# Mirrored angles in the first stage of a one-core vision-transformer tower, and the maximum over the raw output matrix moved to the end of that stage

## The reference, cut to what matters

```python
# stage 1: an S4D kernel for 64 inputs c, 128 channels h, 64 modes n, 1024 steps l
dt = exp(log_dt); A = -exp(inv_A_real) + 1j * A_imag; dtA = A * dt[:, None]
Cc = B * C * (exp(dtA) - 1) / A
K  = 2 * einsum('chn,hnl->chl', Cc, exp(dtA[:, :, None] * arange(1024))).real
h  = K                                             # (64, 128, 1024)
# stage 3, for each of the 64 inputs
h = h + attention(layernorm(h), wq, wk, wv, wo)
h = h + ffn(layernorm(h), W_base, b_base, lora_A, lora_B, router, prior, active)
```

## Time and profile before

| | us |
|---|---|
| median of 3 runs (lowest, highest) | 3096.68 (3093.18, 3097.64) |
| the profiled execution: its time | 3095.41 |
| its span, first to last instruction | 3093.6 |
| stage 1: start to the barrier | 0 to 268.8 |
| stage 2 | 268.8 to 345.9 |
| stage 3 | 345.9 to 3093.6 |

### The profile page before, as it was taken

How to read it: one execution, slowest core, us unless ns; L and a number is a source line. 1 busy time by engine, 2 the same in 40 slices (tenths; PEclk the granted TensorE clock), 3 DMA queues, 4 the chain that set the end, 5 groups by cost and what they waited for, 6 DMA issues and landing times.

```text
span 3093.6 us, 62128 instructions
## 1 busy us (share of the span) xinstructions
PE 2852.0 (92%) x16986; PEld 1418.5 (46%) x16986; DVE 2500.3 (81%) x8865; ACT 1913.8 (62%) x5932; POOL 1966.9 (64%) x1722
## 2 busy tenths in 40 slices
PE   3767469999999999999999999999999999999986
PEld 2556234444444444444444444444444444444442
DVE  8996568888888888888888888888888888888872
ACT  5775356666666666666666666666666666666651
POOL 2441157667777767676777676777776776777762
PEclk9887789999999999999999999999999999999998
DMA  5887166676666666766666666666666666666751
GB/s 160 190 182 176 33 125 142 141 150 148 148 143 146 147 148 141 152 147 147 144 146 148 148 141 152 148 148 143 146 145 147 143 150 146 150 142 149 140 125 52
DMA packets 1269008, 442.53 MB, mean 143 GB/s; under 512 B 1200048, under 2 KB 1241264, under 8 KB 1268800
## 3 DMA queue, kind: packets, MB, share of 16 engines
q1 hardware_dynamic: 1268800, 440.62, 65.2%
HBM read 88.15 MB, written 67.11 MB: 50 GB/s over the span
## 4 chain that ended last, share of the span: by engine, by line
PE 38%; DVE 19%; issue 13%; POOL 10%; ACT 7%; DMA 1%; DVEq 0%; ACTq 0%; POOLq 0%; SPq 0%
PE bank_b L1437 18%; PE bank_a L1437 13%; DVE heads L1258 6%; DVE probs L1204 5%; ACT probs L1079 5%; POOL p_hl L1004 4%; POOL probs L1000 3%; PE bank_c L1437 3%; PE score L1408 2%; POOL rope_a L1010 2%; DVE share L1213 2%; POOL xy_hl L1019 1%; PE pv L1426 1%; DVE r L1286 1%; DVE zs L1366 1%
## 5 line engine op out<-in xcount | busy, mean ns | idle before, releaser
L1079 ACT ACTIVATE probs<-probs,negmax 128x128 f32<-128x128 f32 x2048 | 789.7, 387 | 268.9 <-DVE negmax L1204 268.9
L1004 POOL TENSOR_TENSOR p_hl<-probs,p_hl 128x512 f16<-128x512 f32 x512 | 614.9, 1201 | 354.6 <-ACT p_hl L1088 352.3
L1000 POOL TENSOR_TENSOR probs<-probs,rsum 128x512 f32<-128x512 f32 x512 | 556.7, 1087 | 221.7 <-DVE rsum L1215 220.1
L1437 PE MATMUL bank_a<-qkv_hi,xt 128*128 128x512 f16 x2048 | 655.7, 382 | 28.9 <-DMA xt<-xy_hl 28.9
L1204 DVE CUSTOM_DVE_ANT_0 probs<-score,table,scal 128x128 f32<-128x128 f32 x2048 | 596.5, 347 | 58.2 <-issue 56.9
L1437 PE MATMUL bank_b<-b_hi,yt 128*128 128x512 f16 x2048 | 643.1, 381 | 0.0
L1088 ACT ACTIVATE p_hl<-probs 128x512 f16<-128x512 f32 x512 | 319.8, 625 | 424.7 <-POOL probs L1000 417.2
L1258 DVE TENSOR_TENSOR heads<-rope_a,heads 128x512 f16<-128x512 f32 x320 | 402.4, 1273 | 36.5 <-ACT heads L1109 36.5
L1437 PE MATMUL bank_a<-qkv_lo,xt 128*128 128x512 f16 x1024 | 390.7, 381 | 0.0
L1437 PE MATMUL bank_b<-b_lo,yt 128*128 128x512 f16 x1024 | 390.0, 381 | 0.0
L1437 PE MATMUL bank_b<-o_lo,at_hi 128*128 128x512 f16 x1024 | 388.9, 380 | 0.0
(11 more groups left out here) (199 smaller groups left out, 4525.2 us busy)
## 6 DMA issues: line engine op xcount, KB each, us to landing
tok_h<-kout SPq DMA_DIRECT2D x64, 512.0 KB, 5.9
hin<-tok_h SPq DMA_DIRECT2D x64, 512.0 KB, 3.3
r<-tok_h SPq DMA_DIRECT2D x64, 512.0 KB, 3.5
out_dram<-r SPq DMA_DIRECT2D x64, 512.0 KB, 2.9
probs_t<-p_hl SPq DMA_TRANSPOSE x512, 2.8
xc<-in_x_dram SPq DMA_DIRECT2D x32, 128.0 KB, 4.7
raw_a<-in_L_attn_wq_dram SPq DMA_DIRECT2D x1, 4096.0 KB, 14.4
raw_b<-in_L_attn_wo_dram SPq DMA_DIRECT2D x32, 128.0 KB, 3.8
```

The lines of the kernel that those rows point to most:

```text
L1000: TT(x, x, rsum[:, u % 4].unsqueeze(2).to_broadcast([P, GR, T]), ALU.mult).then_inc(s_norm, 1)
L1004: TT(p_hl[:, u % 2, 1], probs[:, u % 4], p_hl[:, u % 2, 0], ALU.subtract).then_inc(s_plo, 1)
L1079: ins = A(probs[:, u % 4, g], probs[:, u % 4, g], ACT.Exp, bias=negmax[:, u % 4, g:g + 1], scale=-1.0, accum_out=sums[:, u % 4, g:g + 1])
L1437: ins = MM(bank, x(c), w[:, c, cols], start=(c == 0 and i == 0), stop=(c == KC - 1 and i == 2))
```

## The change

Four things change together.

1. **Mirrored angles.** The angle of a step is now taken from the middle of its part. Steps 127.5 + x and 127.5 - x have the same cosine and opposite sines, so `k` and `u` and the sine cover only the 128 upper steps (x = 0.5 to 127.5), and `v` is multiplied in two instructions: the upper half by `u`, the lower half by `u` read backwards and by a sign per partition. The table of parts is turned to the middles, for which all four parts now need a factor (before, part 0 had none), so the first tables have 10 rows of turns in place of 8 and factors 256 wide in place of 192.
2. **Order of the parts.** The parts are kept as 0, 2, 1, 3, so that partition half `e` of the products holds parts 2e and 2e+1, which lie side by side in `tok_h`: a store writes runs of 512 numbers (2 KB) where it wrote runs of 256 (1 KB). The bytes are the same.
3. **Loads of `wo`.** Four a chunk in chunks 0 to 7, none in chunks 8 to 15.
4. **Maximum over `raw_b`.** DVE takes it after its last chunk of stage 1 and POOL reduces it there; stage 2 no longer does.

```diff
+PART = (0, 2, 1, 3)
+LH = L0 // 2
+    c[0::2, C_SIGN] = 1
+    c[1::2, C_SIGN] = -1
+    c[:, C_HALF:C_HALF + L0 // 2] = np.arange(L0 // 2)[None, :] + 0.5
...
-        out_v = tok_h.rearrange("c h (q e l) -> e c h q l", e=2, l=L0)
+        out_v = tok_h.rearrange("c h (e q l) -> e c h q l", e=2, l=L0)
...
-                if exists(ch):
-                    load_wo(2 * ch)
-                    load_wo(2 * ch + 1)
+                if exists(ch) and ch < HQ // 4:
+                    for h in range(4 * ch, 4 * ch + 4):
+                        load_wo(h)
...
-            for m in range(1, L1):
-                step(TS(turns[:, 2 * m], turns[:, 0], float(m * L0), None, ALU.mult))
-                step(TS(turns[:, 2 * m + 1], turns[:, 0], float(m * L0), 0.25, ALU.mult, ALU.add))
+            for i in range(L1):
+                middle = PART[i] * L0 + LH - 0.5
+                step(TS(turns[:, 2 * i + 2], turns[:, 0], middle, None, ALU.mult))
+                step(TS(turns[:, 2 * i + 3], turns[:, 0], middle, 0.25, ALU.mult, ALU.add))
...
-                        ins = TS(k[:, h], const[:, C_L0:C_L0 + L0], tabc[:, nxt, NT - 1, h:h + 1],
+                        ins = TS(k[:, h], const[:, C_HALF:C_HALF + LH], tabc[:, nxt, NT - 1, h:h + 1],
                                  const[:, C_Q:C_Q + 1], ALU.mult, ALU.add)
...
-                        ins = STT(u[:, nxt, h], const[:, C_L0:C_L0 + L0], tabc[:, nxt, NT - 1, h:h + 1], k[:, h],
+                        ins = STT(u[:, nxt, h], const[:, C_HALF:C_HALF + LH], tabc[:, nxt, NT - 1, h:h + 1], k[:, h],
                                   ALU.mult, ALU.subtract)
...
-                    TT(v[:, r], v[:, r], u[:, r], ALU.mult).then_inc(s_v, 1)
+                    upper, lower = v[:, r, :, LH:L0], v[:, r, :, 0:LH]
+                    TT(upper, upper, u[:, r], ALU.mult)
+                    STT(lower, u[:, r, :, ::-1], const[:, C_SIGN:C_SIGN + 1], lower, ALU.mult, ALU.mult).then_inc(s_v, 1)
...
             V.tensor_reduce(w["mx"][:, 0:1], part_max[:, :], AX_X, ALU.max).then_inc(w["s_mx"], 1)
+            dve.wait_ge(w["wo_in"], 16 * HQ)
+            V.tensor_reduce(w["mx"][:, 1:2], w["raw_b"][:, :, :], mybir.AxisListType.XY, ALU.max,
+                            apply_absolute_value=True).then_inc(w["s_mx"], 1)
...
-            dve.wait_ge(s_in[1], 16 * HQ)
-            absmax(1, raw_b[:, :, :])
```

More of the change, by code:

```diff
@@ L43 @@
 C_ONE = C_OWN + 1
-C_ALL = C_ONE + 1
+C_SIGN = C_ONE + 1
+C_HALF = C_SIGN + 1
+C_ALL = C_HALF + L0 // 2
 def constants():
@@ L83, in token_kernel @@
         re = sb("re", [P, NS])
-        turns = sb("turns", [P, 8, NS])
-        whole = sb("whole", [P, 8, NS])
+        turns = sb("turns", [P, 2 + 2 * L1, NS])
+        whole = sb("whole", [P, 2 + 2 * L1, NS])
         sines = whole
@@ L88, in token_kernel @@
         th = sb("th", [P, NS])
-        wmag = sb("wmag", [P, L1 - 1, NS])
-        wre = sb("wre", [P, L1 - 1, NS])
-        wim = sb("wim", [P, L1 - 1, NS])
+        wmag = sb("wmag", [P, L1, NS])
+        wre = sb("wre", [P, L1, NS])
+        wim = sb("wim", [P, L1, NS])
+        g0 = sb("g0", [P, 2, NS])
         gre = sb("gre", [P, L1, NS])
@@ L102, in token_kernel @@
         xs = sb("xs", [P, 2, CH // 2, NS, 2])
-        u = sb("u", [P, 2, CH, L0])
-        k = sb("k", [P, CH, L0], I32)
+        u = sb("u", [P, 2, CH, LH])
+        k = sb("k", [P, CH, LH], I32)
         qb = sb("qb", [P, 1])
@@ L110, in token_kernel @@
         tmp = spare[:, 0, 0:18 * NS].rearrange("p (i n) -> p i n", n=NS)
-        mix = spare[:, 1, 0:18 * NS].rearrange("p (i m n) -> p i m n", i=6, n=NS)
+        mix = spare[:, 1, 0:6 * L1 * NS].rearrange("p (i m n) -> p i m n", i=6, n=NS)
         part_max = sb("part_max", [P, NCH])
@@ L248, in _ @@
             chunks(pool, body)
-            pool.wait_ge(w["s_mx"], 1)
-            nc.gpsimd.partition_all_reduce(w["mxa"][:, 0:1], w["mx"][:, 0:1], P,
-                                           bass.bass_isa.ReduceOp.max).then_inc(w["s_all"], 1)
+            for i in range(2):
+                pool.wait_ge(w["s_mx"], i + 1)
+                nc.gpsimd.partition_all_reduce(w["mxa"][:, i:i + 1], w["mx"][:, i:i + 1], P,
+                                               bass.bass_isa.ReduceOp.max).then_inc(w["s_all"], 1)
         @block.scalar
@@ L264, in _ @@
             step(nc.scalar.activation(th[:, :], re[:, :], ACT.Tanh, scale=0.5))
-            for m in range(1, L1):
-                step(nc.scalar.activation(wmag[:, m - 1], re[:, :], ACT.Exp, scale=float(m * L0)))
-            act.wait_ge(s_dt, 12)
+            for i in range(L1):
+                step(nc.scalar.activation(wmag[:, i], re[:, :], ACT.Exp, scale=float(PART[i] * L0)))
+            act.wait_ge(s_dt, 14)
             step(nc.scalar.activation(sines[:, :, :], turns[:, :, :], ACT.Sin, scale=TURN))
@@ L336, in _ @@
             step(TT(turns[:, :, :], turns[:, :, :], whole[:, :, :], ALU.subtract))
-            dve.wait_ge(s_at, 8)
+            dve.wait_ge(s_at, 9)
             t = [tmp[:, i] for i in range(18)]
@@ L362, in _ @@
             step(STT(t[1], t[16], 2.0, bi, ALU.mult, ALU.mult))
-            step(TT(gre[:, 0], t[0], t[1], ALU.add))
+            step(TT(g0[:, 0], t[0], t[1], ALU.add))
             step(STT(t[2], t[15], 2.0, bi, ALU.mult, ALU.mult))
             step(STT(t[3], t[16], 2.0, br, ALU.mult, ALU.mult))
-            step(TT(gim[:, 0], t[2], t[3], ALU.subtract))
-            sc = sines[:, 2:2 * L1].rearrange("p (m a) n -> p a m n", a=2)
+            step(TT(g0[:, 1], t[2], t[3], ALU.subtract))
+            sc = sines[:, 2:2 * L1 + 2].rearrange("p (m a) n -> p a m n", a=2)
             step(TT(wim[:, :], wmag[:, :], sc[:, 0], ALU.mult))
             step(TT(wre[:, :], wmag[:, :], sc[:, 1], ALU.mult))
-            g0r = gre[:, 0:1].to_broadcast([P, L1 - 1, NS])
-            g0i = gim[:, 0:1].to_broadcast([P, L1 - 1, NS])
+            g0r = g0[:, 0:1].to_broadcast([P, L1, NS])
+            g0i = g0[:, 1:2].to_broadcast([P, L1, NS])
             step(TT(mix[:, 0], g0r, wre[:, :], ALU.mult))
             step(TT(mix[:, 1], g0i, wim[:, :], ALU.mult))
-            step(TT(gre[:, 1:L1], mix[:, 0], mix[:, 1], ALU.subtract))
+            step(TT(gre[:, :], mix[:, 0], mix[:, 1], ALU.subtract))
             step(TT(mix[:, 2], g0r, wim[:, :], ALU.mult))
             step(TT(mix[:, 3], g0i, wre[:, :], ALU.mult))
-            step(TT(gim[:, 1:L1], mix[:, 2], mix[:, 3], ALU.add))
+            step(TT(gim[:, :], mix[:, 2], mix[:, 3], ALU.add))
             step(V.tensor_copy(tab_c[:, 0, 0:L1], gre[:, :]))
@@ L572, in _ @@
             nc.gpsimd.memset(keep["shift"][:, :], LSHIFT).then_inc(s_cst, 1)
[L574 to L578, removed]
+            pool.wait_ge(s_lmx, 1)
+            nc.gpsimd.partition_all_reduce(mxa[:, 2:3], mx[:, 2:3], P, bass.bass_isa.ReduceOp.max).then_inc(s_all, 1)
+            pool.wait_ge(s_lmx, 3)
             nc.gpsimd.partition_all_reduce(mxa[:, 3:5], mx[:, 3:5], P, bass.bass_isa.ReduceOp.max).then_inc(s_all, 1)
```

## The result

The changed kernel takes 3110.59 us (median of 5 runs, 3110.21 to 3114.82), the kernel before 3096.68: ratio 1.0051, interval 1.0036 to 1.0066. It is 14 us slower, where 23 us less were forecast.

| | stage 1 | stage 2 | stage 3 | two inputs in stage 3's loop | span |
|---|---|---|---|---|---|
| before | 268.8 | 77.1 | 2747.7 | 82.58 | 3093.6 |
| changed | 260.0 | 71.4 | 2777.4 | 83.60 | 3108.8 |
| difference | -8.8 | -5.7 | +29.7 | +1.02 | +15.2 |

A forecast was written before the change was run, and what follows sets the result against it. DVE was taken to bound stage 1, with a two-chunk loop through PE next. Stage 1's 18.4 us and stage 2's 4.8 off 3095.4 gave 3072.2, as a median 3073.5; range 3064 to 3082.

The forecast's parts named there:

- 89% of the span is the third, which the change leaves alone: Stage 3: taken as untouched by the change, so no time gained or lost there.
- The chance of 0.95 for faster: Whole kernel: faster than before 0.95, same 0.02, slower 0.03.
- Stage 1: 8.8 us in place of 18.4: Stage 1 as a whole: forecast 18.4 us shorter, ending at 247.9.
- the loop over two chunks closes at kps: Stage 1: DVE's `z` waits for PE's products in every second chunk, 2 to 3 us each.
- the tail: End of stage 1, from v(14) to the end of ACT's copies: 23.0 us, bounds 22.0 and 24.4.
- The pair: Stage 1, two chunks of the loop: 14.27 + 11.75 = 26.0 us, seven such pairs up to v(14).
- The products: Stage 1, PE's kps that close the loop: the slow kind at 1.2 GHz, 9.3 us.
- DVE's own part: Stage 1, DVE's work from the start of one `z` to the end of the next `v`: from 13.66 to 11.75 us.
- Both rivals on it: Stage 1, `u` read backwards: half rate, +7.6 us, 3081, chance 0.10; far more, slower than before, chance 0.04.
- Stage 2: 5.7 us in place of 4.8: Stage 2 without the maximum over `raw_b`: 4.8 us gained, limited by the load of `W_base`; bounds 4.8 and 5.86.
- The transfers: Stage 1, first half: longer runs make stores cheaper, near 6.3 us; sum 11.4 us a chunk, nothing waits, cost 0.
- the rival: Stage 1, transfers bound the first half: 13.2 us a chunk against 13.0, +2 to +5 us, 3076 to 3078, chance 0.14.

The follow-up runs named there:

- a_pad4: The changed kernel with four one-column memsets added on DVE at the end of stage 1: 3058.32 us, ratio 0.9878 to the kernel before.
- b_max: The kernel before with only the moved maximum over `raw_b` and its loads, four a chunk in the first half; angles unchanged: 3091.95 us, ratio 0.9982.

## Why the prediction was wrong

**The step that failed** is in the first paragraph: "89% of the span is the third, which the change leaves alone". The change left its lines alone, not its place in DVE's instruction stream: ten instructions more ahead of it brought the stall of each pass from 0.54 to 1.63 us (28 and 27 times) and stage 3 29.7 us, more than the whole gain. The signs were there to read: an "issue" wait of DVE once a pass ahead of `share`, 15.2 us in 28 times, tied to no engine. No rival had it. The chance of 0.95 for faster stood on causes that all lie in stages 1 and 2. Without that loss the time would have been 3096.7 - 14.5 = 3082 us, at the far end of the range even so, since stage 1 gave 9.6 us less than forecast (below).

That the stall is DVE's wait for instructions rests on four findings: it depends on the count of DVE instructions alone; the old time is back 128 instructions further on; it stands at one place of the program; and in all passes but the odd one it ends 1.7 to 2.1 us after a transfer of instructions has started. Ten instructions more between the loop's head and the boundary hide about 1 us of that.

The Trainium skill ("Runtime: NRT & Kernel Launch", Instruction fetch mechanics) says that a taken branch to a page that is no longer held forces a fetch before execution can go on. The runs agree in kind, with a stall of up to 2.1 us behind the back branch. The same section of the Trainium skill gives a block of 256 instructions in 16 KB; here 128 more instructions give back the old time, and the transfers have half that size. At 12 instructions between head and boundary the price over 968 was 0.84 us a pass, at 2 it was 1.9. Why it vanishes at 968 is worked out from the counts: the loop then ends at 968 + 379 = 1347, ahead of the boundary at 966 + 3 x 128 = 1350, so it lies in three blocks of 128, and at every other count tried in four. That it needs no transfers there is seen; what DVE holds of its program is not.

**Stage 1: 8.8 us in place of 18.4.** The mechanism was right (the loop over two chunks closes at kps, `z` waits 2.8 us in every second chunk, predicted "2 to 3"; PE stood idle 5.7 us ahead of these products, predicted 5.9), and so was the tail (v(14) ends at 234.35, ACT's last copy at 257.41: 23.06, predicted 23.0). The pair was sized too small, 27.3 for 26.0, in two terms:
- The products: 10.19 us against 9.3. I took kps(2) alone; in the same trace kps(8) took 10.20 after 4.48 of idle. The length of the wait alone does not say how long a burst takes: in a_pad4 the products took 8.86 us after 2.59 of idle and 7.17 after 2.88. What else sets it, no run here shows. Its first pair, closed by products of 8.86, took the 26.0 us forecast (57.54 to 83.53 on DVE), the next, closed by 10.14, took 27.3, and so did all behind it. So 26.0 could be had, for one pair; that the loop would settle on the slow kind was not in the forecast.
- DVE's own part: 12.19 against 11.75. `k` took 2.14 to 2.31, not 1.77: for 1024 columns less it lost 0.54 us, half of what the reduction's price per column gives. `u` was right at 2.19.

7 x 1.3 = 9.1, and v(0) ended at 43.28, not 42.9: together the 9.5 us by which v(14) is late.

**Reading backwards** cost at most 0.06 us: 1.28 us for `v`'s lower half, with one operand more, against 1.22. Both rivals on it fall.

**Stage 2: 5.7 us in place of 4.8**, within the bounds given (4.8 and 5.86), for the reason given: the next wait is that for `W_base`.

**The transfers** were hidden as forecast, for the wrong reason. I had halved the price of a store for its longer runs. Two pairs of late chunks, with the same `xc` loads and no `wo` loads: first b_max (1 KB runs), then the changed kernel (2 KB runs), DMA share and GB/s last:

```profile
184.40:212.00 27.60, 18.92 (x82) 15.94 (x81) 27.46 (x43) 22.28 (x37) 11.39 (x6) 0.88 0.71 172
```

```profile
194.88:222.15 27.27, 19.41 (x82) 15.95 (x81) 24.32 (x44) 20.03 (x37) 11.33 (x7) 0.87 0.67 165
```

27.6 x 0.71 = 19.6 against 27.27 x 0.67 = 18.3: hardly less: with the 2.1 us of the `xc` loads taken off, 16.2 for the stores of a pair against 17.5, not half. The rule of the Trainium skill ("DMA: Bandwidth & Descriptors", Specifications) that runs of 512 B and more go at line rate agrees with this better than my estimate did. The first half then needs what the rival said:

```profile
58.34:85.66 27.32, 19.38 (x82) 15.93 (x81) 24.32 (x45) 20.02 (x37) 11.45 (x7) 0.88 0.99 212
```

27.3 x 0.99 / 2 = 13.5 us a chunk, of 13.65, and still ACT waited for no store there: the angles with two loads a chunk had no shorter stage 1 (258.8 against 257.8). A share of 0.99 of the DMA engines is full, but not late.

## What to carry to other kernels

A long loop on an engine can stall for its own instructions behind the back branch; an edit anywhere ahead of it, in code that runs once, moves that stall. Count the engine's instructions ahead of the loop before and after an edit, look for "issue" waits that come once a pass, and compare two versions of a kernel at the same count modulo 128, else, as here, 50 us of chance lie over 15 of effect. The number of instruction transfers in the profile tells the good place from the others: 48 against 183. Here four memsets make the changed kernel 1.2% faster than before (3058.32, 0.9878), and 14 of them make the old one 0.8% faster with no other edit.

Where a loop of waits closes over an engine whose clock falls and rises, take its time from all its occurrences in the trace, and carry the slowest: the new loop settled on the slowest kind.

## What the runs showed of the hardware

- Stage 3 took 2778, 2727 and 2747 us with 964, 968 and 954 DVE instructions ahead of it, and 2747 with 1082.
- Its loop of 379 DVE instructions drew five instruction transfers of 8.2 KB a pass, and next to none where it began at 968; the stall behind the back branch ended 1.7 to 2.1 us after one of them had started.
- 32 products took 10.2 us after 3.97 us of idle and 8.86 after 3.93, and 8.86 after 2.59 where 2.88 gave 7.17: the low clock is not a matter of the idle time alone.
- A DVE operand read backwards cost no more than 0.06 us on 1024 columns, with a third operand besides.
